# Half of the k copy moved from ScalarE to VectorE in a 1-core Flamingo-style kernel, and a changed tail

## The reference

```python
for i in range(6):                              # x: 4 x 512 x 128
    x = attn_layer(shift_tokens(x), ...) + x
    x = ffn_layer(shift_tokens(x), ...) + x
def attn_layer(x, Wqkv, qs, ksc, Wo):
    q, k, v = split(x @ Wqkv)                   # 16 heads of 64
    q, k = l2norm(q) * qs, l2norm(k) * ksc
    q, k = rotary(q), rotary(k)                 # cos and sin with a scale
    out = local_attention(q, k, v)              # windows of 32, keys of this and the last window
    return out @ Wo
def ffn_layer(x, ...):
    xn = layernorm(x)
    a, gate = split(xn @ W1 + b1)               # 341 wide each
    return a * gelu(gate) @ W2 + b2
```

## Time and profile before

| | |
|---|---|
| median of 3 runs | 1777.94 us (1777.28 to 1783.73) |
| profiled execution: its time, its span | 1781.41 us, 1779.4 us |
| PE busy | 1709.0 us, 96% of the span |
| DVE busy | 1370.6 us, 77% |
| ACT busy | 1396.2 us, 78% |
| POOL busy | 1499.9 us, 84% |
| chain that ended last, by engine | PE 75%, ACT 13%, POOL 5%, issue 4%, DVE 3% |
| mean granted TensorE clock | 0.986 |

### The profile page before, as it was taken

The page is one execution under the profiler, slowest core; times in us unless marked ns, Lnnn a source line. Parts: engine busy times, 40 slices in busy tenths (PEclk is TensorE's granted clock), DMA queues, the critical chain, the costliest instruction groups (busy, mean ns, idle before and its releaser), DMA issues.

```text
span 1779.4 us, 48666 instructions
## 1 busy us (share of the span) xinstructions
PE 1709.0 (96%) x18122; PEld 1136.8 (64%) x18122; DVE 1370.6 (77%) x2399; ACT 1396.2 (78%) x2746; POOL 1499.9 (84%) x1204
## 2 busy tenths in 40 slices
PE   8689999999999999999999999999999999999996
PEld 7356666666666666666666666666666666666663
DVE  5687877778778777877887778787777877877773
ACT  3577878878779788788788787887887887877862
POOL 4799898888888988988988889889889888888860
PEclk8899999999999999999999999999999999999998
DMA  4022222222322223222223222222222222222221
GB/s 117 21 75 74 74 63 70 62 74 72 84 60 71 68 57 82 74 69 73 66 61 85 66 74 74 59 61 78 77 73 64 72 61 60 60 71 58 58 65 30
DMA packets 155273, 120.59 MB, mean 68 GB/s; under 512 B 42607, under 2 KB 151457, under 8 KB 154913
## 3 DMA queue, kind: packets, MB, share of 16 engines
q1 hardware_dynamic: 155041, 117.48, 24.9%
HBM read 18.79 MB, written 1.05 MB: 11 GB/s over the span
## 4 chain that ended last, share of the span: by engine, by line
PE 75%; ACT 13%; POOL 5%; issue 4%; DVE 3%; ACTq 0%; DVEq 0%; POOLq 0%
PE qk_bank L374 13%; PE ring_bank L470 9%; PE sc_bank L421 8%; PE ring_bank L446 8%; PE ring_bank L387 7%; PE ring_bank L514 5%; PE ring_bank L459 5%; PE ring_bank L434 5%; PE ring_bank L408 4%; PE ring_bank L525 4%; PE ring_bank L397 3%; ACT sq L616 2%; ACT L718 2%; POOL turned L1047 2%; POOL turned L1054 2%
## 5 line engine op out<-in xcount | busy, mean ns | idle before, releaser
L1047 POOL TENSOR_TENSOR turned<-qkn,tables 128x512 f32<-128x512 f32 x384 | 490.4, 1277 | 162.1 <-DVE qkn L844 159.3
L1054 POOL TENSOR_TENSOR turned<-qkn,tables 128x512 f32<-128x512 f32 x384 | 498.2, 1297 | 0.0
L374 PE MATMUL qk_bank<-wqkv,xT 128*128 128x512 f32 x768 | 363.5, 596 | 4.4 <-DVE qkn L852 4.4
L827 DVE TENSOR_REDUCE ss<-sq 128x16 f32<-128x1024 f32 x192 | 234.0, 1219 | 116.9 <-ACT sq L616 116.6
L1083 POOL TENSOR_TENSOR turned<-turned 128x512 f32<-128x512 f32 x192 | 254.6, 1326 | 15.1
L892 DVE TENSOR_TENSOR o<-ring_bank,rr 128x512 f32<-128x512 f32 x192 | 132.6, 691 | 169.1 <-PE ring_bank L446 167.6
L1090 POOL TENSOR_TENSOR turned<-turned 128x512 f32<-128x512 f32 x192 | 244.5, 1273 | 15.0
L692 ACT ACTIVATE oT<-ring_bank 128x512 f32<-128x512 f32 x192 | 114.5, 596 | 179.5 <-PE ring_bank L459 179.3
L446 PEld LDWEIGHTS ring_bank<-vw,pT 128*32 128x32 f32 x6144 | 156.7, 110 | 143.7 <-issue 143.6
L656 ACT ACTIVATE kB<-ring_bank 64x512 f32<-64x512 f32 x384 | 225.8, 588 | 23.4 <-PE ring_bank L408 21.2
L421 PE MATMUL sc_bank<-kB,qT 128*32 128x128 f32 x6144 | 204.1, 273 | 8.9 <-ACT qT L647 8.9
(11 more groups left out here) (170 smaller groups left out, 2975.2 us busy)
## 6 DMA issues: line engine op xcount, KB each, us to landing
vw<-vs SPq DMA_DIRECT2D x1152, 64.0 KB, 2.0
vw<-vs SPq DMA_DIRECT2D x672, 32.0 KB, 1.9
wqkv<-in_L_ffn_Wqkv_dram SPq DMA_DIRECT2D x20, 384.0 KB, 3.5
wo<-in_L_ffn_Wo_dram SPq DMA_DIRECT2D x20, 128.0 KB, 3.3
w<-in_L_ffn_W_dram SPq DMA_DIRECT2D x6, 341.0 KB, 3.3
wqkv<-in_L_ffn_Wqkv_dram SPq DMA_DIRECT2D x1, 1536.0 KB, 10.3
x<-in_x_dram SPq DMA_DIRECT2D x2, 512.0 KB, 4.4
out_dram<-x SPq DMA_DIRECT2D x4, 256.0 KB, 2.3
```

What stands on the lines that cost most here:

```text
L374: mm = pe.matmul(QK[u % 2][:, i * UW:(i + 1) * UW], tok, wqkv[:, layer % 2, cut:cut + UW], start=True, stop=True)
L827: dve.tensor_reduce(ss[:, u % 2, :], heads(sq[:, :]), AX.X, ALU.add).then_inc(ss_done, 1)
L1047: return pool.tensor_tensor(heads(turned[:, u % 2, 2 * i, :]), heads(qkn[:, u % 2, i * UW:(i + 1) * UW]), table.unsqueeze(1).to_broadcast( ...
L1054: return pool.tensor_tensor(halves(turned[:, u % 2, 2 * i + 1, :]), halves(qkn[:, u % 2, i * UW:(i + 1) * UW])[:, :, ::-1, :], table.rearr ...
```

## The change

The k copy is split. ScalarE copies the even heads (partitions 0 to 63) and signals `k_low`; VectorE waits for `k_low`, copies the odd heads (partitions 64 to 127) as the last stage of its slot, and only this frees the ring bank. The scores wait for the k copy too. Four edits concern the last slots: the transpose of the results and VectorE's `finish` move from slot s=0 (TensorE) and s=1 (VectorE) to s=1 and s=2; `add_ffn` goes ahead of `sum_squares` in slots s=0; the squares of the very last unit go ahead of ScalarE's copies of o, p and k; and TensorE multiplies a constant tile into a free bank 8 and 18 times in two places of the last group (`keep_warm`).

```diff
@@ TensorE
+                pe.wait_ge(*evicted("k", u))          # in scores(u)
...
+            def keep_warm(g, n):
+                if g != GROUPS - 1:
+                    return
+                pe.wait_ge(qn_done, UNITS)
+                for _ in range(n):
+                    pe.matmul(QK[0][:, 0:P], mean_w[:, :], mean_w[:, :], start=True, stop=True)
...
                 transpose_o(n - 6)
+                if s == 1:
+                    transpose_out(g - 3)
                 transpose_p(n - 4)
...
                 if s == 3:
+                    keep_warm(g - 2, 18)
                     up("gate", 1, g - 2, 0)
...
                 if s == 1:
+                    keep_warm(g - 2, 8)
                     variance(g - 2)
...
-                if s == 0:
-                    transpose_out(g - 3)
                 transpose_q(n - 2)
@@ ScalarE
-            def copy_kB(u):
+            def copy_k_low(u):
...
                 act.wait_ge(ring_made[i % RINGS], i // RINGS + 1)
-                for h in range(2):
-                    ev = act.activation(kB[64 * h:64 * h + 64, HP * half:HP * half + HP, h, WIN + P * t:WIN + P * t + P],
-                                        RING[i % RINGS][64 * h:64 * h + 64, :].rearrange("p (k q) -> p k q", q=P), ACT.Copy)
-                ev.then_inc(ring_read[i % RINGS], 1)
+                act.activation(kB[0:64, HP * half:HP * half + HP, 0, WIN + P * t:WIN + P * t + P],
+                               RING[i % RINGS][0:64, :].rearrange("p (k q) -> p k q", q=P), ACT.Copy).then_inc(k_low, 1)
...
                 copy_v(n)
+                if n == UNITS - 1:
+                    squares(n)
                 copy_oT(n - 6)
                 copy_pT(n - 4)
...
-                copy_kB(n - 2)
-                squares(n)
+                copy_k_low(n - 2)
+                if n < UNITS - 1:
+                    squares(n)
@@ VectorE
+            def copy_k_high(u):
+                if not 0 <= u < UNITS:
+                    return
+                g, layer, b, t, half = place(u)
+                i = turns["k", u]
+                dve.wait_ge(k_low, u + 1)
+                dve.tensor_copy(kB[64:128, HP * half:HP * half + HP, 1, WIN + P * t:WIN + P * t + P],
+                                RING[i % RINGS][64:128, :].rearrange("p (k q) -> p k q", q=P)
+                                ).then_inc(ring_read[i % RINGS], 1)
...
                 if s == 1:
-                    finish(g - 3)
                     centre(g - 2)
                 if s == 2:
+                    finish(g - 3)
                     add_eps(g - 2)
...
-                sum_squares(n - 1)
                 if s == 0:
                     add_ffn(g - 3)
+                sum_squares(n - 1)
...
                 if s == 3:
                     layer_norm(g - 2)
                     sum_p(n - 4)
+                copy_k_high(n - 2)
```

More of the change, by code:

```diff
@@ L230, in build @@
         k_summed = sem("k_summed")
+        k_low = sem("k_low")
         sc_open = sem("sc_open")
@@ L821, in _ @@
                     normalise(b - 1, row, x_nat, b_stat, b_rstd, b_x)
+            dve.wait_ge(zero_ready, 2)
             def sum_squares(u):
```

## The result

The changed kernel takes 2193.32 us in the median (2184.66 to 2197.19, 4 runs), the kernel before 1778.47 us (4 runs): a ratio of 1.231, 95% interval 1.2288 to 1.2333. It is 415 us slower; 350 had been forecast.

The account below looks back on a forecast made before the run. TensorE, busy 96%, was taken as the bound. Net +10.85 and 4.15 us a group made +15.0, +355 over 189 slots; with -5 for the tail, 1781.4 became 2131, median near 2128 us, range 2030 to 2210.

Parts of the forecast that it names:

- The mechanism: VectorE's late copy holds the next slot's scaling queued behind it, and TensorE's projections wait for that scaling, once a slot.
- The chain from T: From the end of k's transpose through both half copies, `newton`, `scale_k` and `scale_q` to the projections: 3.5 us.
- The direct waits: TensorE's new waits ahead of the projections for the scaling of q, in six of eight slots: 12.05 us a group.
- The later waits: Further TensorE waits because VectorE's whole slot comes 3.1 us later (`layer_norm`, ring banks, ScalarE): 4.15 us a group.
- the old 1.2: TensorE's waits in the kernel before, about 1.2 us a group, mostly ScalarE's and expected to go.
- the gate products' slot: Slots s=3: `layer_norm` was ready only 0.23 us ahead of the gate products, so 1.6 us more wait.
- the prediction's own signs of being wrong: VectorE starting its slot before k's transpose ends, copy under 0.4 or over 0.9 us, or steady granted clock leaving 1.00.
- a rival with 0.13: TensorE's clock falls in the new gaps: 2173 us if in s=0 alone, 2280 if in all five long waits; chance 0.13.
- only the direct chain costs: Rival: waits beyond those of the projections are absorbed; +10.85 us a group, about 2029 us; chance 0.17.
- it is not slower: Rival: the late copy is hidden and the waits of the kernel before go, about 1745 us; chance 0.04.
- The relief of ScalarE: Taking half the k copy off ScalarE can save only TensorE's present waits, about 1.2 us a group, some 28 us.
- The tail: Edits of the last slots: -2.6 us in the last up products, -2.4 from reordering; -5, between 0 and -8.

Follow-up runs that it names:

- experiment 5: Changed kernel plus constant products ahead of the transposes of q, 8 in slots s=1, 4, 5 and 12 in s=0: 2133.03 us, ratio 1.1974.
- experiment 8: Changed kernel with VectorE's copy moved into the next slot, behind `less_maxima` and `centre`, tail edits included: 1774.95 us against 1781.32 before, ratio 0.9956.
- experiment 10: Kernel before with only the split copy, placed in the next slot behind `less_maxima` and `centre`, no tail edits: 1772.88 us against 1780.01, ratio 0.9967.
- experiment 2: Changed kernel with only the edits of the last slots, ScalarE copying both halves of k as before: 1778.92 us against 1780.63, ratio 0.9982.

## Why the prediction was right, and where its sizes were off

- **The mechanism** was right: copy, then the queue behind it, then the projections. The chain from T measured 3.37 us, 3.5 had been summed: ScalarE's start and half as taken, the copy 0.695 for 0.68, and `newton` to `scale_q` 1.78 rather than 1.96, as `newton`'s first instruction took 0.18 here and 0.36 in the row that I had used.
- **The direct waits**: 12.05 us a group forecast; the list has 245.0 us over 143 waits, 10.4 a group over 23.6 groups. Each is some 0.2 to 0.5 smaller than its forecast: in the group around 1200 us they are 2.78 in s=0 (forecast 3.2), 1.90 in s=1 (2.35), 1.15 in s=3 (1.5), 2.01 and 1.94 in s=4 and s=5 (2.25 each) and 0.29 in s=7 (0.5).
- **The later waits**: 4.15 forecast. From 14.4 of waits a group by experiment 5, and the 10.4 less the old 1.2, some 5.2 is left for them. The slots of experiment 5 against those before say where, in medians: beyond their direct waits s=3 grew by 1.8 us, s=0 by 0.9, s=4 and s=5 by 0.5 to 0.6 each, s=7 by 0.3, 4.4 in all with the small ones. So the gate products' slot came near its forecast of 1.6, although the list books only 20.5 us in 24 times, 0.85 each, on `xnT`. How the rest divides among the ring banks and engines was not taken apart.
- **Luck**: these two errors go opposite ways, 1.65 too much and some 1 too little. That the waits came out at 14.4 for a forecast of 15.0, and experiment 5 at 2133 for a sum of 2128, owes something to that.
- **The term that was missing is the clock.** That it leaves 1.00 in the steady part was one of the prediction's own signs of being wrong, and it did. The forecast gave it to a rival with 0.13 and argued that gaps of about 2.2 us are harmless, since one of 2.39 us had been. This step failed: the fall came after a gap of 2.01 us. It cost 60 us (experiment 5), nearly the whole distance between 2128 and 2193. The Trainium skill, "TensorE: Matmul & The Clock Gate", section "HAM oscillation — how this bites in real kernels", has the clock fall again and again where gaps between bursts recur; this trace agrees, with 0.957 over the run and 0.51 in the stretch above. The gaps of that section's example are of 3 to 5 us, though, and here some of 1.6 to 2.8 us were enough. By that rule I had expected the fall in slots s=0. It came there in 7 of 21 groups (from 250 us on), and in the others, as in the group above, it did not.
- **The rivals.** That only the direct chain costs fell (2029 forecast, 2193 measured). That it is not slower would have needed another place for the copy; experiment 8 shows that place, and that there the net loss of 415 us is gone.
- **The relief of ScalarE** was put at the 1.2 us a group of old waits, 28 us at most; 6 us came of it (experiment 10), a fifth of that ceiling. The ceiling was not far off: in the kernels of experiments 8 and 10 slots s=1 and s=4 gain 0.92 us a group between them, but s=3 gives 0.58 back to the copy's new place.
- **The tail** was put at -5. By itself it is worth 3 us (experiment 2). In the changed kernel it does not show: from the start of the last projection matmul to the end of the span it is 82.7 us (2109.3 to 2192.0), where it was 76.5 before. In its chain stand

```profile
2125.98 4.82 issue
2130.80 1.94 PE ring_bank L448 x32
...
2177.05 5.40 PE ring_bank L523 x12
```

so the up products did gain their 2.35 us, but TensorE idled 4.82 us ahead of an `attend`, and the stretch 2132 to 2136 had a granted clock of 0.75. That this wait is for the mean's bank, freed by `centre` on the late VectorE (which ends at 2130.70), I read from the order of the instructions; it was not tried apart.

## What to carry to other kernels

Ask of a moved instruction not how long it runs and how idle its new engine is, but when its input is ready and what stands behind it in the queue: the same 0.7 us copy, with what the change gave elsewhere already taken off, cost 415, 162, 76 or no us at four places in VectorE's order. The good place here is behind the scaling, the maxima and `centre`, for which others wait, and early enough for the copy's own reader in all slots but s=3; places further back were not tried. TensorE at the bound had a second price for being made to wait, since its clock fell in some of the gaps. That price could be measured by filling them, with fillers no longer than the gap: with 16 products in place of 8 or 12 the kernel took 104 us more (2237 against 2133).

## What the runs showed of the hardware that was not expected

- A gap's length alone did not tell whether TensorE's clock falls. In the changed kernel a gap of 2.01 us was followed by a granted clock of 0.51 and projections of 3.68 us, and in another group one of 2.00 us by projections of 1.98. The longest gap, 2.78 us, was harmless in 14 of 21 groups, and the slot after the harmless 2.00 had the fall behind 1.62; of nine such gaps of 1.60 to 1.62 us, eight were followed by slow projections:

```profile
1123.89 1.98 PE L375 MATMUL qk_bank<-wqkv,xT 128*128 128x512 f32 x4 [2.00 <-DVE qkn L876]
...
1133.45 3.34 PE L375 MATMUL qk_bank<-wqkv,xT 128*128 128x512 f32 x4 [1.62 <-DVE qkn L876]
...
1165.81 1.98 PE L375 MATMUL qk_bank<-wqkv,xT 128*128 128x512 f32 x4 [2.78 <-DVE qkn L876]
```

- VectorE's copy of 64 x 512 from PSUM takes 0.694 to 0.696 us, as long as two-operand instructions of 128 x 512 (0.68 to 0.69): at this width half the partitions save nothing.
- VectorE's small `newton` instructions differ between the kernels: L833 had 0.319 us in the median and up to 1.247 before, and the same instruction 0.176 in the median in the changed kernel, where GpSimd often stands idle at that point (in the slot s=5 above for 3.60 us up to 1219.71). That GpSimd is the reason was not tried.
